# The rope's multiplications of the short tiles: VectorE or GpSimd behind a ScalarE copy

## The reference

```python
q = jnp.einsum('bim,ghmd->bghid', x, w_aq); k = jnp.einsum('bim,gmd->bgid', x, w_ak)
even, odd = jnp.split(x, 2, axis=-1)                      # inside _rope
return jnp.concatenate([even * cos - odd * sin, even * sin + odd * cos], axis=-1)
s = jnp.einsum('bghid,bgjd->bghij', q * qk_mult, k * qk_mult)   # then mask, softmax, times v, w_ao
```

## Time and profile before

| | |
|---|---|
| median of 3 executions | 1148.86 us (1147.38 to 1149.29) |
| the profiled execution | 1148.7 us, span of its instructions 1147.1 us |
| mean granted PE clock | 0.965 of full speed |
| busy: PE, DVE, ACT, POOL | 90%, 54%, 46%, 34% of the span |
| attention | until about 1000 us; batch 1's first score near 500 us |
| short tiles | until about 174 us, and from about 498 to 664 us |

### The profile page before, as it was taken

The page is one execution under the profiler, slowest core; times in us unless marked ns, Lnnn a source line. Parts: engine busy times, 40 slices in busy tenths (PEclk is TensorE's granted clock), DMA queues, the critical chain, the costliest instruction groups (busy, mean ns, idle before and its releaser), DMA issues.

```text
span 1147.1 us, 16798 instructions
## 1 busy us (share of the span) xinstructions
PE 1032.7 (90%) x5472; PEld 746.7 (65%) x5472; DVE 622.3 (54%) x1613; ACT 524.8 (46%) x1162; POOL 392.3 (34%) x417
## 2 busy tenths in 40 slices
PE   5789999999999999988899999999999999566825
PEld 4667776777777767666677767777777676444412
DVE  5556655456665665636575553556756655322206
ACT  4435445455454554533354464554545545132312
POOL 4213234535233441032322344252333411134642
PEclk9999999999999999998999999999999999878967
DMA  9501010000000000000000000000000083987458
GB/s 294 153 19 46 17 42 5 26 5 21 5 5 24 5 17 5 5 18 10 21 21 10 19 7 16 11 15 6 6 15 5 2 200 88 228 264 144 56 99 309
DMA packets 67316, 65.00 MB, mean 57 GB/s; under 512 B 10545, under 2 KB 61605, under 8 KB 67232
## 3 DMA queue, kind: packets, MB, share of 16 engines
q1 hardware_dynamic: 53856, 51.85, 16.2%
q0 software_dynamic: 9216, 6.76, 3.9%
q10 hardware_dynamic: 4160, 5.31, 1.4%
HBM read 40.83 MB, written 36.44 MB: 67 GB/s over the span
## 4 chain that ended last, share of the span: by engine, by line
PE 73%; DVE 8%; DMA 7%; issue 6%; POOL 3%; ACT 2%; SPq 1%; ACTq 0%; POOLq 0%; DVEq 0%
PE o_ps L925 20%; PE s_ps L901 16%; PE ring L876 11%; PE ring L914 10%; PE ring L940 8%; DMA sums<-erow,goal_u 5%; PE ring L882 3%; SPq L607 1%; PE s_ps L904 1%; PE ring L931 1%; DVE q_sin L1085 1%; POOL slot_rows L679 1%; POOL q_rot L667 1%; DVE neg_max L1101 1%; DVE q_cos L1083 1%
## 5 line engine op out<-in xcount | busy, mean ns | idle before, releaser
L925 PE MATMUL o_ps<-pt,v_sb 128*128 128x512 f32 x576 | 294.6, 594 | 2.9 <-DVE ot L1129 2.0
L772 ACT ACTIVATE pt<-ring 128x512 f32<-128x512 f32 x288 | 171.0, 594 | 263.2 <-PE ring L914 252.3
L764 ACT ACTIVATE probs<-s_ps,neg_max 128x128 f32<-128x128 f32 (+7 forms) x256 | 189.5, 741 | 151.9 <-DVE neg_max L1101 143.3
L1101 DVE TENSOR_REDUCE neg_max<-s_ps 128x1 f32<-128x128 f32 (+7 forms) x256 | 191.5, 751 | 95.8 <-PE s_ps L904 93.9
L914 PE MATMUL ring<-ident,probs 128*128 128x128 f32 x1152 | 174.6, 274 | 6.1 <-ACT probs L764 5.7
L901 PE MATMUL s_ps<-kt_hi,qt_hi 128*128 128x512 f32 (+3 forms) x384 | 165.1, 430 | 0.0
L914 PEld LDWEIGHTS ring<-ident,probs 128*128 128x128 f32 x1152 | 128.4, 141 | 54.3 <-issue 53.4
L667 POOL TENSOR_TENSOR q_rot<-q_cos,q_sin 128x256 f32<-128x256 f32 x80 | 64.1, 802 | 224.3 <-DVE q_sin L1085 221.1
L679 POOL DMA_INDIRECT slot_rows<-row,slot_u x96 | 97.6, 1017 | 109.8 <-DVE slot_u L1227 85.4
L901 PE MATMUL s_ps<-kt_hi,qt_lo 128*128 128x512 f32 (+3 forms) x384 | 133.3, 347 | 0.0
L901 PE MATMUL s_ps<-kt_lo,qt_hi 128*128 128x512 f32 (+3 forms) x384 | 132.9, 346 | 0.0
(11 more groups left out here) (160 smaller groups left out, 1442.0 us busy)
## 6 DMA issues: line engine op xcount, KB each, us to landing
fsum<-sums SPq DMA_DIRECT2D x32, 256.0 KB, 6.8
sums<-blank SPq DMA_DIRECT2D x16, 384.0 KB
wexp<-in_L_ffn_w_gate_dram SPq DMA_DIRECT2D x32, 192.0 KB, 7.8
wexp<-in_L_ffn_w_up_dram SPq DMA_DIRECT2D x32, 192.0 KB, 7.8
wexp<-in_L_ffn_w_down_dram SPq DMA_DIRECT2D x32, 192.0 KB, 8.4
slot_rows<-blank SPq DMA_DIRECT2D x1, 5184.0 KB, 28.8
srow<-slot_rows ACTq DMA_DIRECT2D x1, 2592.0 KB, 22.3
x_sb<-in_L_attn_x_dram SPq DMA_DIRECT2D x16, 128.0 KB, 2.1
```

Source lines behind the costliest of these rows:

```text
L764: act.activation(probs[:, u % 2, h, 0:blocks(u) * P], s_ps[:, n % 2, score_cols(n)], ACT.Exp, bias=neg_max[:, n % 8:n % 8 + 1], accum_out= ...
L772: reader(act.activation(pt[:, n % PTB, :], bank(s), ACT.Copy), s)
L925: pe.matmul(o_ps[:, :], v_sb[:, j, g * D:(g + 1) * D], pt[:, n % PTB, :], start=(j == 0), stop=(j == blocks(u) - 1)).then_inc(pv_done, 1)
L1101: dve.tensor_reduce(neg_max[:, n % 8:n % 8 + 1], s_ps[:, n % 2, score_cols(n)], AX_X, ALU.max, negate=True).then_inc(max_ready, 1)
```

## The change

POOL_TILES becomes all eight tiles of a batch, so the 40 ropes of the short tiles take the form of the long ones. Nothing else in the text is changed; the order SEQ, the places in BETWEEN and the buffers stay. DVE's branch with L1083 and L1085, its waits among them, is not taken any more; that is also the only place where an engine waited for the tables.

```diff
-POOL_TILES = range(4, NT)
+POOL_TILES = range(NT)
```

## The result

The changed kernel takes 1192.6 us (1190.1 to 1194.3); the kernel before took 1149.1 us beside it. The ratio is 1.0375 (95% interval 1.0359 to 1.0391): 3.75% slower, +43.5 us. The forecast was 1187 us, between 1170 and 1201.

What follows compares the result with a forecast made beforehand. It took PE, 90% busy, to be bound in short tiles by waits for POOL's q_rot. 1148.7 us plus spans 35.4, start 2.6 and clock 3.4, less gains 3.4, made 1187 us; range 1170 to 1201.

Steps and rivals of the forecast that it cites:

- the wait for q_rot: Sign: PE's wait at L882 for POOL's q_rot grows from 13.0 to about 50 us, in some 25 waits.
- DVE's 55 us: Sign: DVE's busy time falls by 55 us, from two PSUM multiplications removed in each of 40 ropes.
- the tiles 1: Sign: each tile 1 becomes about 6 to 8 us longer.
- The route: Short-tile ropes: projection to q_rot takes 4.84 us, 4.99 to PE's transposes, against 2.96 to PE before.
- The sum over the spans: Short tiles: each rope costs max(0, 4.99 - PE span); 17.0 and 18.4 us by batch, together 35.4 us.
- ACT's order: At each projection ACT is free for the copy, except at 108.80 and 509.44, where the ends coincide; no cost.
- The sharing with VectorE: GpSimd and VectorE contend for SBUF; in steady short tiles this adds next to nothing, as DVE's big operations read PSUM.
- The start: First three ropes of tile 0 (K, 0, 1), a chain of their own: 2.6 us late, between 1.2 and 4.0.
- The clock: PE's granted clock falls after some two or three idle gaps: 3.4 us, of 0 to 12.
- The gains: Small PE waits that shrink, for q_sin's ring bank, chose, probs and the row at 518: 3.4 us.
- The rival that half would be absorbed: Time lost at a rope is given back within the tile, leaving 15 to 25 us: 1164 to 1174; chance 0.15.
- Faster: Rival: DVE's relief wins, 1135 us at best, some 1144 for the short tiles' part; chance 0.04.

Runs made afterwards that it cites:

- The pad: The kernel before with two idle GpSimd multiplications ahead of q_rot in the 40 short-tile ropes: 1187.0 us, ratio 1.0322.
- the run with longer spans: The changed kernel with other places in BETWEEN, for tiles 1 and 2 above all, so that spans on PE grow: 1176.3 us, ratio 1.0229.
- half of the way: The kernel before with short tiles in mixed form: ACT copies to q_cos, DVE multiplies sines from PSUM, POOL the cosines: 1167.2 us, ratio 1.016.
- hidden ropes: The change only for 12 short-tile ropes whose PE span was over 5 us, the other 28 in VectorE's form: 1149.1 us, ratio 0.9989.
- tiles 2 and 3: The change only in tiles 2 and 3 of each batch, tiles 0 and 1 staying in VectorE's form: 1166.4 us, ratio 1.0134.
- the second of the runs with longer spans: The kernel before with some transposes and projections one head later, in tile 0 only: 1152.7 us, ratio 1.0026.
- the fillers: The changed kernel with 4 to 12 idle matmuls on PE ahead of its q_rot wait at 19 exposed ropes: 1184.3 us, ratio 1.0301.

## Why the prediction was right, and where its terms were off

The mechanism and its place were as forecast: DVE, ACT and POOL have room, the latency of the rope sets most of the loss, the long tiles last as long as before (the lateness is 27.1 us at tile 3 and at tile 7). The pad shows that a longer rope makes 37.8 us with DVE and ACT left as they were, the run with longer spans that the same work loses 16.3 us less. Of the signs named, the wait for q_rot came (54.0 us in 28 waits, for about 50 in 25), DVE's 55 us did not (35), and the tiles 1 became 9.2 and 3.6 us longer instead of 6 to 8 each. By the steps:

- **The route.** 4.84 us was read from the long tiles, 4.79 to 4.85 were found at the exposed ropes where the copy started at once. Right to 0.05 us.
- **The sum over the spans** was 17.0 and 18.4 us without the first three ropes. In the parts that the clock left alone it holds rope for rope: tile 2's K, 1 and 2 came 1.66, 1.90 and 1.46 us late against 1.67, 1.90 and 1.48; tile 1's rope 1 2.01 against 2.02; tile 3's rope 1 1.14 against 1.10.
- **ACT's order was misread.** The prediction took ACT to be free at each projection, but for two places. In rope 0 of each tile 3 the copy started 0.9 us late, and the rope came 1.39 us late instead of 0.57, which makes 1.6 us for the two batches. ACT in the changed kernel:

```profile
...
158.97 0.58 ACT L764 ACTIVATE probs<-s_ps,neg_max 128x384 f32<-128x384 f32 x1 [1.54 <-DVE neg_max L1101]
...
159.54 0.59 ACT L737 ACTIVATE q_cos<-ring 128x512 f32<-128x512 f32 x1
...
```

  An exp (L764) stands ahead of the copy (L737) in ACT's order and waits for neg_max on DVE, and the copy waits with it. The trace of the kernel before has the same exp, with the same wait, behind the end of the same projection (133.70+0.40 = 134.10). PE and ACT before:

```profile
...
133.70 0.40 PE L876 MATMUL ring<-w_hi,xt_lo 128*128 128x512 f32 x1
...
```

```profile
...
134.41 0.58 ACT L764 ACTIVATE probs<-s_ps,neg_max 128x384 f32<-128x384 f32 x1 [1.54 <-DVE neg_max L1101]
134.89 0.19 ACT L764 ACTIVATION_READ_ACCUMULATOR probs<-s_ps,neg_max 128x1 f32 x1
...
```

  So this term could have been read. At 13 of the 40 short ropes the instruction ahead of the copy ended 0.3 to 1.7 us after the projection before the change. That most of them cost nothing after it is luck: PE's new waits let ACT catch up. Once it went the other way, at batch 1's tile 1, K, where ACT was free before and the copy started 1.2 us late.
- **The sharing with VectorE reaches into the steady tiles.** The prediction put it at next to nothing there. The K rope of each tile 3 came 0.6 us late, though its copy started at once and its q_rot was ready 1.2 us ahead. What came late is a small instruction of the router on DVE, L1156, that started while POOL multiplied. After the change (DVE, POOL, PE), then before:

```profile
...
150.96 1.00 DVE L1156 TENSOR_SCALAR sig<-sig 128x160 f32<-128x160 f32 x1 [1.92 <-ACT sig L790]
...
```

```profile
...
150.58 1.28 POOL L664 TENSOR_TENSOR q_sin<-q_cos,sin_sb 128x512 f32<-128x512 f32 x1 [6.62 <-ACT q_cos L737]
...
```

```profile
...
153.80 0.66 PE L914 MATMUL ring<-ident,probs 128*128 128x128 f32 x4 [0.29 <-DVE hid L1162]
...
```

```profile
...
127.18 0.23 DVE L1156 TENSOR_SCALAR sig<-sig 128x160 f32<-128x160 f32 x1
...
```

  DVE's next instructions (L1157 to L1162) follow on it, and PE waits for the last one. The runs agree: the step is 0.6 to 0.7 us where L1156 took 0.88 to 1.01 us at that place (changed kernel, half of the way, hidden ropes, tiles 2 and 3), and none where it took 0.23 (the pad and the second of the runs with longer spans). That makes 1.2 us for the two batches.
- **The start** was sized at 2.6 us, between 1.2 and 4.0, and is 5.7. Two things were mis-sized. The contention: the multiplication in place took 2.13 us beside a w_lo instead of 1.26, here in POOL's and DVE's timelines, and w_lo itself 1.62 instead of the 1.22 of the earlier trace rows:

```profile
...
19.35 2.13 POOL L666 TENSOR_TENSOR q_cos<-q_cos,cos_sb 128x512 f32<-128x512 f32 x1
...
36.31 1.26 POOL L666 TENSOR_TENSOR q_cos<-q_cos,cos_sb 128x512 f32<-128x512 f32 x1
...
```

```profile
...
18.73 1.62 DVE L1038 TENSOR_TENSOR w_lo<-probs,w_hi 128x1024 fp32r<-128x1024 f32 x1 [4.28 <-ACT w_hi L708]
...
```

  That happened once in each of the three ropes, 0.85 us each time, and once more in an addition (1.71 us instead of 0.72), so 3.5 us of the 4.5 between my replay (25.8 for the third rope) and the trace (30.3). The Trainium skill (GPSIMD Engine Reference, Specifications) says that the two engines contend when the VectorE instruction is in a 2-port perf mode or has two SBUF inputs, as w_lo has; the trace agrees. I took half of that contention where all of it came, and once more than I had counted. The upper bound of 4.0 left out the clock: from 18 to 28 us PE ran at the lower level, and the third rope waited for transposes that ran at it. That this makes the last 1.0 us is not shown.

```profile
...
18.00:28.00 10.00, 6.20 (x19) 4.64 (x17) 5.71 (x5) 4.51 (x7) 8.39 (x6) 0.50 1.08 338
...
```

  ACT's queue stood as worked out, three weight splits and kt_hi behind the copy that waits for the K rope, with 4.20 us of idling before it:

```profile
...
17.16 0.60 ACT L737 ACTIVATE q_cos<-ring 128x512 f32<-128x512 f32 x1 [4.20 <-POOL q_rot L668]
17.65 2.94 ACT L708 ACTIVATE w_hi<-probs 128x1024 fp32r<-128x1024 f32 x3
20.49 0.59 ACT L708 ACTIVATE kt_hi<-ring 128x512 fp32r<-128x512 f32 x1
24.03 0.60 ACT L737 ACTIVATE q_cos<-ring 128x512 f32<-128x512 f32 x1 [2.95 <-POOL q_rot L668]
...
```

- **The clock** was sized at 3.4 us of 0 to 12 and took 6 to 8. After the change most of tile 0 and 1 of batch 0 runs at the lower level, since gap follows on gap; I had counted gaps one by one. The steps of the changed kernel in batch 0 exceed the latency term by 1.3, 0.5, 1.9 and 1.6 us at tile 0's ropes 2 and 3 and tile 1's K and 0, 5.2 us, and with the fillers these four together exceed it by nothing. Another 1.6 us at batch 1's tile 0, rope 2, looked the same to me, but the fillers took only 0.6 of it.
- **The gains** were put at 3.4 us. Found: -0.8 and -0.5 us at rope 3 of tiles 1 and 2 in both batches, -0.9 at batch 1's tile 1, rope 2, -0.4 at rope 0 of batch 1's tile 0, and tile 2's rope 0, forecast 0.85 late, came 0.2 us early in both batches. With 0.9 at the rope behind the scatters and 0.8 at batch 1's tile 1, K, that is 7.7 us. I had left out a wait of PE of 0.76 us for a pt copy in each tile 2, which is not in the trace any more; I take it that the wait at its K rope covers it.
- **DVE's busy time** was to fall by 55 us and fell by 35. The multiplications took 55 us as worked out, but other instructions grew: a scaling of the router (L1156) took 623 ns on the mean before and takes 863 now, the addition L1224 went from 204 to 310, the conversion L1227 from 172 to 261. The traces show with what: in both, L1156 took 0.23 to 0.25 us where no product of POOL ran, and 1.00 to 1.01 us where it started during one, 8 times before the change and 13 times after. What it costs PE is seen at tile 3's K rope (above); at tile 2's PE waits for q_rot anyway. These instructions don't add up to the whole 20 us.

```profile
...
L1156 DVE TENSOR_SCALAR sig<-sig 128x160 f32<-128x160 f32 x16 | 13.8, 863 | 28.5 <-ACT sig L790 28.5
...
L1224 DVE TENSOR_TENSOR taken<-taken,chose 128x64 bf16<-128x64 bf16 x16 | 5.0, 310 | 0.1
...
L1227 DVE TENSOR_SCALAR slot_u<-slot 128x8 uint32<-128x8 f32 x16 | 4.2, 261 | 0.6
...
```

So the sum in the traces is 35.4 (spans) + 5.7 (start) + 6.8 (clock, with the 1.6 that are not proven) + 2.9 (tile 3: ACT's order 1.6, L1156 1.2) - 7.7 (gains) = 43.1 us, against 35.4 + 2.6 + 3.4 + 0 - 3.4 = 38.0. The lateness was shared out over the terms rope by rope, so that they add up is no test of them; the pad, the fillers and the longer spans are. Start, clock and tile 3 cost 9.4 us more than forecast, and the gains are 4.3 us larger, which hides nearly half of that: the large term was right by its working, that the total came within 5.5 us is in part luck.

The rival that half would be absorbed is refuted: nothing is given back in the long tiles, and even if all 7.7 us of gains were counted as absorbed, that is a fifth of the latency term. "Faster" needed a route of 2.96 us.

## What to carry to other kernels

Before moving a step to engines with room, measure the span that the bottleneck has between the step's input and its output at every place where it occurs, and set the new route's latency against each; where other places already use the new route, its latency can be read there. A form that is free where spans are long costs its full difference where they are short, so choose the form by place and not by engine load. Read in the trace of before where the instruction ahead of the new one in its engine's order ends, at every place. Look at which instructions of VectorE will run beside new work on GpSimd, the small ones too. Where PE is the bottleneck and waits again and again, as here for 2 to 4 us, count the clock as well, and try filler matmuls in the wait: they are a cheap experiment, and here they gained 0.6% without the change.

## What the runs showed of the hardware

- Idle matmuls in PE's waits made the kernel before 7.6 us faster (0.6%) with no other change: the granted clock between 8 and 100 us went from 0.96 to 1.00, and the steps gained in its trace, which ends 4.7 us earlier (1.0 us at tile 0's rope 3, 1.0 and 1.3 us at batch 1's tile 1) stand where the lower level had been. The last two came in the run with only hidden ropes too, without fillers, when the level stayed up by itself.
- The same gap on PE was followed by the lower level in one execution and not in another. In the runs with VectorE's form at tile 1's K rope the trace has a step of 1.6 us there twice (the runs with only hidden ropes, and with tiles 2 and 3), with a grant of 0.77 and 0.82 instead of 1.00 in 40 to 44 us. A single execution scatters by such steps, in both directions.
- GpSimd and VectorE hold each other up when both work on SBUF: a GpSimd product of 512 elements (per partition) took 2.13 instead of 1.26 us beside a VectorE subtraction of 1024 with both inputs in SBUF, and that one 1.62 instead of 1.22. The small VectorE instructions wait for the whole product: all 13 times that L1156 started during one, it ended 0.10 us after the product did, 1.00 us after its start instead of 0.25. It has one input tensor, in SBUF. L1227 took 0.89 instead of 0.17 us, and L1224 up to 1.27 instead of 0.18, in the same way. The maximum over 128 columns of PSUM (L1101) was not held up: 0.28 to 0.29 us beside a product, 0.26 to 0.29 without one.
